# Weight scales from sums of squares, edge keys ahead of the zeros, and edge counts put together between products

## The reference

```python
def reference(x, src, dst, ...):                    # x: 1250 x 1024, 20000 edges
    xn = _layernorm(x, axis=-1)
    x = x + _L0_gnn_ref(xn, src, dst, ...) + _L0_mix_ref(xn[None], ...)[0]
    x = x + _L0_ffn_ref(_layernorm(x, axis=-1)[None], ...)[0]

def _L0_gnn_ref(x, edge_src, edge_dst, ...):        # two layers; deg_inv = 1 / max(in-degree, 1)
    msg = h[edge_src]; agg = segment_sum(msg, edge_dst, N); mean = agg * deg_inv[:, None]
    h = relu(x @ W_self0 + mean @ W_neigh0 + b0);  out = h @ W_self1 + mean(h) @ W_neigh1 + b1

def _L0_mix_ref(x, ...):                            # fmap(t) = elu(t) + 1
    Q = fmap(x @ Wq + bq); K = fmap(x @ Wk + bk); value = x @ Wv + bv
    KV = sum(K * value, axis=1); Ksum = sum(K, axis=1)
    out = gelu(((Q * KV) / (Q * Ksum + 1e-6)) @ Wo + bo)

def _L0_ffn_ref(x, w_gate, w_up, w_down):           # three products with weights of 4 bits, and
    ...                                             # five roundings by the maximum of a whole tensor
```

## Time and profile before

| | us |
|---|---|
| time, median of 3 runs (1313.82 to 1317.33) | 1316.98 |
| the profiled execution, its own time | 1314.77 |
| its span, first to last instruction | 1312.9 |
| PE busy | 1165.0 (89%) |
| DVE busy | 747.7 (57%) |
| POOL busy | 383.6 (29%) |
| ACT busy | 284.2 (22%) |

### The profile page before, as it was taken

One profiled execution on the slowest core, in us unless ns is written; L12 is line 12 of the kernel. 1 busy time (PEld: TensorE's weight loads), 2 busy tenths in 40 slices (PEclk: granted clock), 3 DMA queues, 4 the chain that ended last, 5 costly groups with the idle time before them and its releaser, 6 DMA issues.

```text
span 1312.9 us, 15359 instructions
## 1 busy us (share of the span) xinstructions
PE 1165.0 (89%) x6350; PEld 627.0 (48%) x6350; DVE 747.7 (57%) x1265; ACT 284.2 (22%) x308; POOL 383.6 (29%) x214
## 2 busy tenths in 40 slices
PE   3899099999999999945995999999999999959948
PEld 2455055545555554422442455444444445448924
DVE  7587198878675473404363445675655345652663
ACT  4431022122122132102210101122210012232530
POOL 2003776576777773787300000000000000000000
PEclk9999599999999999977997999999999999979979
DMA  8097235533433339411566023513131040000004
GB/s 245 16 406 225 60 50 147 162 51 69 85 59 60 85 66 309 97 2 17 195 255 216 0 91 107 166 51 123 47 115 49 17 160 1 0 0 1 1 23 135
DMA packets 139278, 130.20 MB, mean 99 GB/s; under 512 B 74732, under 2 KB 113644, under 8 KB 137672
## 3 DMA queue, kind: packets, MB, share of 16 engines
q1 hardware_dynamic: 72648, 128.77, 28.6%
q0 software_dynamic: 66560, 0.44, 5.1%
HBM read 101.19 MB, written 27.65 MB: 98 GB/s over the span
## 4 chain that ended last, share of the span: by engine, by line
PE 46%; DMA 20%; issue 13%; POOL 11%; DVE 7%; ACT 1%; SPq 1%; POOLq 0%; DVEq 0%; ACTq 0%
PE ps L946 20%; DMA at_scratch<-copies,cell 13%; POOL at_scratch L569 11%; PE ps L1005 7%; PE ps L977 6%; PE ps L1027 6%; PE ps L1047 3%; DMA raw<-in_L_gnn_W_neigh_dram 3%; DMA key_scratch<-key_r 2%; DVE key_b L1128 1%; DMA parts<-at_scratch 1%; DVE AT L1142 1%; PE ps L862 1%; PE ps L852 1%; PE ps L993 1%
## 5 line engine op out<-in xcount | busy, mean ns | idle before, releaser
L875 PE MATMUL ps<-xnT,whl 128*128 128x512 f16 (+1 forms) x2160 | 384.7, 342 | 35.8 <-DVE whl L1110 35.8
L569 POOL DMA_INDIRECT at_scratch<-copies,cell x160 | 339.7, 2123 | 169.5 <-issue 88.6
L875 PEld LDWEIGHTS ps<-xnT,whl 128*128 128x128 f16 x2160 | 211.5, 98 | 208.7 <-DVE whl L1110 36.5
L946 PE MATMUL ps<-hb,hT 128*128 128x512 f16 x960 | 209.0, 379 | 1.4 <-DVE hT L1404 1.4
L946 PEld LDWEIGHTS ps<-hb,hT 128*128 128x128 f16 x960 | 93.6, 98 | 112.6 <-DVE hT L1404 1.8
L553 POOL PARTITION_ALL_REDUCE ag<-am x9 | 5.7, 638 | 446.6 <-DVE am L1496 235.0
L946 PE MATMUL ps<-hb,VT 128*128 128x512 f16 x480 | 106.4, 385 | 33.1 <-DVE x_acc L1359 31.6
L946 PE MATMUL ps<-hb,xnT 128*128 128x512 f16 x480 | 104.1, 379 | 0.0
L946 PEld LDWEIGHTS ps<-hb,VT 128*128 128x128 f16 x480 | 47.4, 99 | 92.0 <-DVE x_acc L1359 32.1
L1005 PE MATMUL ps<-P,AT 125*128 125x512 f16 x400 | 87.8, 379 | 0.0
L977 PE MATMUL ps<-AT,P 125*128 125x512 f16 (+1 forms) x480 | 84.7, 339 | 0.0
(11 more groups left out here) (207 smaller groups left out, 1155.4 us busy)
## 6 DMA issues: line engine op xcount, KB each, us to landing
raw<-in_L_gnn_W_neigh_dram SPq DMA_DIRECT2D x32, 512.0 KB, 5.9
parts<-at_scratch SPq DMA_DIRECT2D x20, 625.0 KB, 5.1
raw<-in_L_gnn_W_self_dram SPq DMA_DIRECT2D x24, 512.0 KB, 5.9
at_scratch<-zeros SPq DMA_DIRECT2D x4, 3060.0 KB, 21.8
key_b<-key_scratch SPq DMA_DIRECT2D x8, 1250.0 KB, 10.1
raw<-in_L_mix_Wo_dram SPq DMA_DIRECT2D x16, 512.0 KB, 4.0
x_all<-in_x_dram SPq DMA_DIRECT2D x9, 512.0 KB
x_acc<-in_x_dram SPq DMA_DIRECT2D x9, 512.0 KB
```

The costliest lines, as they stand in the source:

```text
L569: pool.indirect_dma_start(out=at_scr[c % 2][:, :], out_offset=bass.IndirectOffsetOnAxis(ap=cell[:, c:c + 1], axis=0), in_=copies[:, c:c + ...
L875: mm = pe.matmul(acc_of(c)[:, a:b], whl[:, i, wp, k, :], xnT[:, k, ap, a:b], start=(k == 0 and wp == 0 and ap == 0), stop=(k == KC - 1 and ...
L946: mm = pe.matmul(half_bank(i), stationary[:, k, ap, t * TP:t * TP + P], hb[:, n % 2, k, wp, :], start=(k == 0 and wp == 0 and ap == 0), st ...
```

## The change

Seven things, in the order of time.

1. `ident32`, the identity for turning, is no longer made by GpSimd: VectorE writes one column of ones into a 128 x 129 tile of zeros, ScalarE sends it to DRAM, waits, and reads it back with rows of 128, which gives the diagonal. Its two transfers and one wait stand at the start of ScalarE's queue.
2. PE turns all ten tiles ahead of product 0; `columns` is gone.
3. The scale of a weight comes from its sum of squares. ScalarE squares a chunk and sums along the rows (`norms`, four chunks at the start of each group's loop, ahead of the copy of Q), and the rows of whole weights (ring entries "norm" in place of "max", at the same places). A matmul with ones (`sums`, `w_sums`) sums over the partitions. `pow2_norm` makes the power of two. GpSimd takes no part.
4. The keys are made on VectorE behind `chunk_lo(0, 1)`; SP writes and loads them ahead of the zeros. The zeros now go out as 6 transfers for each array, of a tile a third as wide. `load_ahead(4)`, the loads of group 1, stands behind the zeros instead of ahead of them. The scatters into one array wait for the zeros of that array alone.
5. `prepare_scale(g + 2)` and `chunk_lo(g + 1, 0)` on VectorE come behind `k_part(g)` (in group 0 behind `v_part(0)`), not ahead of it; `chunk_hi(g + 1, 0)` on ScalarE moves to the other chunks.
6. GpSimd runs the 160 scatters in one loop, then the b1 sums.
7. `load_parts(s)` stands at tile 11 + 2 s, `counts(s)` behind tile 13 + 2 s. Parts 0 to 5 use the one buffer inside AT's own space and wait for `counts` of the one before; parts 6 to 9 use the other, over `b1_b`, and wait for `b1_ok` once.

`raw_done` becomes one semaphore for each ring slot. The constants 2^-20 and 2^-25 become 2^-15 and 2^-20, since the scales are other powers of two. The diff, cut to its core:

```diff
+        W_SUMS = {9: WN0, 29: WN1, 40: WS1}
+        PART_TILE = {13 + 2 * s: s for s in range(NT)}
         def part_of(s):
-            where = [1 if u in (1, 3, 5) else 0 for u in range(NT)]
-            return where[s], where[:s].count(where[s])
+            return (1, s) if s < 6 else (0, s - 6)
...   # SP
-            load_ahead(4)
-            sp.wait_ge(zeros_set, 1)
-            for b in range(2):
-                for h in range(2):
-                    sp.dma_start(at_scr[b].rearrange("(h p c) o -> h p (c o)", h=2, p=P)[h],
-                                 zeros[:, :]).then_inc(zero_out, 16)
             sp.wait_ge(key_ok, 1)
             sp.dma_start(key_scr.rearrange("(h r e) -> r h e", h=2, e=EP), key_r[:, :, :]).then_inc(key_out, 16)
             sp.wait_ge(key_out, 16)
             load_keys(0)
             load_keys(1)
+            sp.wait_ge(zeros_set, 1)
+            for b in range(2):
+                for h in range(NZ):
+                    sp.dma_start(at_scr[b].rearrange("(h p c) o -> h p (c o)", h=NZ, p=P)[h],
+                                 zeros[:, :]).then_inc(zero_out[b], 16)
+            load_ahead(4)
...   # load_parts
                 if s == 0:
                     for b in range(2):
                         sp.wait_ge(scattered[b], 16 * (ET // 2))
+                elif s == 6:
                     sp.wait_ge(b1_ok, NT)
-                if k > 0:
-                    sp.wait_ge(at_ok, max(u for u in range(s) if part_of(u)[0] == q) + 1)
+                else:
+                    sp.wait_ge(at_ok, s)
...
-                    if n == 2:
-                        load_parts(t)
+                    if NT * n + t + 2 in PART_TILE:
+                        load_parts(PART_TILE[NT * n + t + 2])
                     after_tile(n, t)
...   # GpSimd
-            for n, (g, a, b) in enumerate(TOGETHER):
-                if n >= 3:
-                    scatter(BETWEEN)
-                pool.wait_ge(group_max, n + 1)
-                pool.partition_all_reduce(ma[:, g, a:b], mx[:, g % 2, a:b], P, ABSMAX).then_inc(group_all, 1)
-            scatter(BETWEEN)
-            whole(WO_)
-            scatter(ET)
-            whole(WN0)
+            for c in range(ET):
+                if c % CPP == 0:
                     pool.wait_ge(cell_ok, c // CPP + 1)
+                if c < 2:
+                    pool.wait_ge(zero_out[c], 16 * NZ)
+                else:
+                    pool.wait_ge(scattered[c % 2], 16 * (c // 2))
+                pool.indirect_dma_start(...).then_inc(scattered[c % 2], 16)
...   # ScalarE
+            act.wait_ge(diag_set, 1)
+            act.dma_start(diag_scr.rearrange("(p c) -> p c", p=P), diagonal[:, :]).then_inc(diag_out, 16)
+            act.wait_ge(diag_out, 16)
+            act.dma_start(ident32[:, :], diag_scr[0:P * P].rearrange("(p c) -> p c", p=P)).then_inc(ident_in, 16)
+            def norms(n, of):
+                g, a, b = TOGETHER[n]
+                for i in of:
+                    if i < 4:
+                        r = at["chunk", g, i]
+                        landed(act, r)
+                        ins = act.activation(squared[:, :], raw[:, r % NR, :], ACT.Square,
+                                             accum_out=nq[:, g % 2, i:i + 1])
...
             for g in range(KC):
                 par = g % 2
+                if g + 1 < KC:
+                    norms(g + 2, range(4))
                 act.wait_ge(xn_done, 4 * g + 1)
...   # PE
-            for t in range(5):
+            for t in range(4):
                 turn_xn(t)
...
+            sums(0)
+            for t in range(4, NT):
+                turn_xn(t)
             pe.wait_ge(xt_free, NT)
+            product(0)
+            sums(1)
+            product(1)
...
             for c in range(2, 4 * KC):
                 product(c)
+                g, i = divmod(c, 4)
+                if i == (2 if g == 0 else 1) and g + 1 < KC:
+                    sums(g + 2)
+                if (g, i) == (KC - 1, 0):
+                    w_sums(WO_)
...   # VectorE
             def counts(s):
                 q, k = part_of(s)
+                if s == 6:
+                    dve.wait_ge(at_ok, 6)
...   # groups
-                if g + 1 < KC:
-                    prepare_max(g + 2)
-                    prepare_scale(g + 2)
-                    chunk_lo(g + 1, 0)
-                else:
+                if g + 1 == KC:
                     for j in range(4):
                         job(("half", WO_, 0, j))
                 k_part(g)
-                v_part(g)
+                if g == 0:
+                    v_part(g)
+                if g + 1 < KC:
+                    prepare_scale(g + 2)
+                    chunk_lo(g + 1, 0)
+                if g > 0:
+                    v_part(g)
...
                 behind_tile(i)
+                if i in PART_TILE:
+                    counts(PART_TILE[i])
...
-                if 21 <= i <= 20 + NT:
-                    counts(i - 21)
```

More of the change, by code:

```diff
@@ L306, in build @@
         for k in range(KC):
-            behind(0, k, "max", WN0, k)
+            behind(0, k, "norm", WN0, k)
         for j in range(4):
@@ L588, in _ @@
                 pool.tensor_tensor(x_acc[:TP, t, :], x_acc[:TP, t, :], b1_b[:TP, :], ALU.add).then_inc(b1_ok, 1)
-            for e in (WN1, WS1):
-                whole(e)
             for j in range(NF):
@@ L656, in job @@
                 kind, *of = entry
-                if kind == "half":
+                if kind == "norm":
+                    w, k = of
+                    r = at["norm", w, k]
+                    landed(act, r)
+                    act.activation(raw[:, r % NR, :], raw[:, r % NR, :], ACT.Square,
+                                   accum_out=mw[:, w, k:k + 1]).then_inc(raw_free[r % NR], 1)
+                elif kind == "half":
                     act.wait_ge(so_ok, of[0] + 1)
@@ L680, in _ @@
             deviations(1)
+            norms(0, (0,))
             xn_tile(2)
@@ L683, in _ @@
             turned_hi(2)
+            norms(0, (1,))
             xn_tile(4)
@@ L943, in half_product @@
                         if t == 0 and k % 2 == 0:
[L944 removed]
+                            worked(pe, at["half", w, part, k // 2])
                         for ap, wp in ((0, 0), (0, 1), (1, 0)):
@@ L1431, in _ @@
             for i in range(40, 60):
-                p_low(i, 2.0 ** -25)
+                p_low(i, 2.0 ** -20)
+                if i - 1 in W_SUMS:
+                    scaled.add(W_SUMS[i - 1])
+                    weight_scale(W_SUMS[i - 1])
                 turned(i)
```

278 lines of the change are left out of this document (135 added, 143 removed).

## The result

The changed kernel takes 1292.95 us (median of 4 runs, 1292.09 to 1294.05) against 1316.00 for the kernel before (4 runs, 1313.82 to 1317.33): 0.9827 times, interval 0.9809 to 0.9845. Forecast were 1293.0 and a span of 1290.4; the span is 1290.4. The total is right to the microsecond, but by errors that cancel (-6.5 and +9.0, and -2.5 for the rest), and the step to which the forecast gave the gain turns out not to be needed for it.

The account below looks back on a forecast made before the run. The GpSimd scatter chain was taken as the clock of the first 710 us, PE behind it. Terms +4 (last scatter), -24 (to degrees), -3 (clock), +0.5 gave -22.5, span 1290.4; forecast 1293 us, range 1273 to 1310.

Parts of the forecast that it names:

- part 1: Turning ahead of the products: tiles turned at 47 us, products 0 and 1 done at 74, 5 us later than before.
- (+6): Upper bound for the identity's DRAM trip, in us, if its transfers stood behind all that SP has queued.
- part 2: Keys ahead of zeros: group 1's chunks land late, product 2 starts at 91 us, PE idles 17 us ahead of it.
- parts 3 and 4: Scatter chain: first scatter at 128 us, 13 later than before; length 474, last start 602, +4.
- rival (a): Scatters start on time or collide less with loads, 15 us gained: 1278 us; chance 0.17.
- part 5: Weight scales by squares and matmuls: 33.5 us hole goes, products end at 475 to 480, mixer's 19 tiles at 575.
- Rival (c): Square is outside ScalarE's loaded function set, table loads add 6 us to the first scatter: 1299 us; chance 0.07.
- +0.5 for the sums: PE's cost, in us, for three matmuls with ones outside the cover, 0.3 each, with start-up.
- part 6: Counts read between mixer tiles, cut from b1: last scatter to degrees 88 us instead of 111.8, gain 24.
- Behind the degrees: Order unchanged except WS1's squares on ScalarE; without a wait there, higher clock gives -3 us.
- (b): Slow chain of count parts, gain gone from 10.6 us a part; chance 0.06 slower, 0.07 for 1315 us.
- (d): The end does not move since the WN0 wait only changes its name; chance counted within (b).

Follow-up runs that it names:

- e1: Changed kernel with the four loads of group 1 moved ahead of the zeros: 1291.24 us, 0.9802 of the kernel before.
- e2: Changed kernel with the squares of the next group moved behind the exponential of Q on ScalarE: 1290.96 us, 0.9798 of the kernel before.
- e6: Changed kernel with keys turned ahead of product 0 and scatter cells made earlier, so the scatters start earlier: 1259.42 us, 0.9526 of the kernel before.
- e7: Changed kernel with the edits of e6 and e2 together: 1254.25 us, 0.9507 of the kernel before.
- e3: Changed kernel with count-matrix parts read late as before: two buffers, behind the b1 sums, from tile 20 on: 1293.29 us, 0.9814 of the kernel before.
- e9: e3 plus one unused partition_all_reduce on GpSimd ahead of scatter 80: 1306.65 us, 0.9909 of the kernel before.
- e4: Kernel before with only the GpSimd reduction for WN0's maximum moved earlier, behind 24 scatters instead of all: 1315.07 us, 0.9982 of the kernel before.
- e8: e3 with the eight squares of WN1 moved from ScalarE to VectorE: 1312.11 us, 0.9943 of the kernel before.
- e11: e7 with the count-matrix parts read late as in e3: 1255.51 us, 0.9537 of the kernel before.

## Why the prediction was right, point by point

- **Turning and the identity (part 1).** Right: the identity's two transfers are issued at 1.15 and 5.30 and it is used at 10.87, 0.7 us earlier than before, so they did not stand behind all that SP had queued (+6); turned tiles at 46.8 for 47, products 0 and 1 done by 74.8 (85.92 - 11.13) for 74.
- **Keys, zeros, product 2 (part 2).** The mechanism is the forecast's. Its size was 5 us too large: product 2 at 85.9 for 91, with PE idle for 11.1 us and not 17, since the last chunk was there at 83.2, not at 87 to 89.
- **First and last scatter (parts 3 and 4).** 122.4 for 128, the same 5 us; length 473.1 for 474; last start 595.5 for 602. This is the first of the two errors, -6.5. That an earlier start is an earlier end, on which rival (a) rests too, is not borne out at this size: e1 and e2 started the chain another 5 to 7 us earlier and gained nothing that can be measured. Only the 60 us of e6 and e7 came through, for half and more.
- **Scales by products (part 5).** Right: products end at 476.4, PE stops after 19 tiles, for 32.6 us. Rival (c) is false: the only switch of ScalarE's function table between the first tiles and the end of the products is at 85.80, behind Q's copy, for exp, as in the earlier trace rows; the squares at 78 to 84 bring none. The +0.5 for the sums is a slip in the forecast, whose own terms give three times 0.3; the trace has two of them outside the cover, 0.60 and 0.28.
- **Counts (part 6).** Here the second error lies, +9: the rhythm is 9.3 for 8, the upper end of the range, and PE stops 6.8 us ahead of the sums of WN1, whose squares ScalarE can only make when SP has sent the chunks behind the parts. Last scatter to degrees 97.0 for 88. So this step gave 14.8 us (111.8 to 97.0) where 24 were forecast. That much is a size. What fails is the reason, "the gain is what follows" from cutting the parts loose from b1: e3 has them bound to b1 and takes the same time. On after's own path the cut is there (part 0 goes out 3.7 us behind the last scatter's start, not 36.6), but one buffer gives 18.1 of it back, and without the cut the rest of the diff brings as much.
- **Where e3 gains as much.** By its stages against before: 11.4 us from the last scatter to part 0 and 9.2 in the parts. e9 accounts for the first, as the 7.4 us gap, which e4 keeps although it takes the reduction itself (1.1 us) away from there; the rest is the b1 sums themselves, 23.8 us instead of 26.7 (2.4 each instead of 2.65, and 0.9 of waiting for a tile less). e8 accounts for the second, and more. This explains e3. For after, whose parts 0 to 5 don't wait for b1, the gap would not count (e9 above), and the place of WN1's squares was not undone. Both were in the diff, and the forecast priced both at nothing: it counted squares and maxima by busy time, off the path, and read the 7.41 in the earlier trace rows as part of "b1 from 608".
- **Behind the degrees.** -5.0 for -3: the twenty matmuls take 4.48 for 7.48 (forecast 4.3). The other 2.0 lie in the feed-forward part, where matmuls behind two waits took 6.63 for 8.17 and 41.10 for 41.90, and were not forecast. The clock in 690 to 720 is 1.00 of full, so at the upper of the two levels, where PE had been working on; before it was 0.72, behind the 14 us wait. The windows of after and before, start and end, length, busy by engine, clock, DMA share, GB/s:

```profile
690.00:720.00 30.00, 30.00 (x146) 14.12 (x145) 12.14 (x11) 5.72 (x8) 0.00 (x0) 1.00 0.21 74
```

```profile
690.00:720.00 30.00, 15.93 (x61) 6.49 (x60) 9.88 (x14) 3.27 (x4) 0.00 (x0) 0.72 0.67 237
```

- **Rivals.** (b) was half there (rhythm 9.3, its threshold 10.6). (d) is true of the WN0 wait (e4) and, against the forecast, of the early parts too, as long as the rest of the diff is there (e3).

Open: why the chain of the scatters grows when it starts 5 to 7 us earlier (e1, e2), and why the same order can differ by 8 us from one execution to the next (e7, e11). The change's own parts "squares on ScalarE" and "no reductions" were each undone alone, on e3's base; neither was tried alone on the kernel before, and neither was undone in the changed kernel with its parts early. The early parts were not tried alone on the kernel before either.

## What to carry to other kernels

Price a moved instruction by what it waits for and what is queued behind it, not by its duration: eight operations of 1.2 us cost 12 us between the parts since each stood in line for a load. Ask of a long wait what is late next before you promise its length: here 31.6 us (e4) and 11 us (e1, e2) were worth nothing that could be measured, and what moved the end was starting the chain of scatters 60 us earlier. Before a shift of a few microseconds in one profile is explained, look where it arises: the 8 us between e7 and e11 stood there long before the orders differ. Look for idle time of GpSimd that ends by "issue" where its kind of work changes: in e9 a single partition reduction cost 6.7 us before it and 7.5 us ahead of the next ordinary operation, 240 us later.

## What the runs showed of the hardware

- GpSimd stands 6.7 us ahead of a first `partition_all_reduce` and 7.1 to 7.5 us ahead of the next `tensor_tensor`; the indirect transfers between them stand for nothing of the kind, and the second gap comes all the same (e9, e4).
- An indirect transfer that adds 125 single elements goes out every 2.3 us where it waits for no earlier one to land and every 2.98 us on average over the chain of after (473.1 for 159). Beside the zeros and the chunks behind them it was 5.4 us (62.67 to 100.25 for seven, e6).
- With zeros queued, one load of 512 KB held SP's queue for 17.7 us at its issue (54.72 in after). The issue of a transfer can be the wait, and everything behind it on that engine waits too.
